# TensorE multiplies ones while the first weights are loaded and ahead of the first queries

## The chip, the cores and the metric

The kernel runs on one core of a Trainium2 chip. The metric is the device time of one execution in microseconds (us); smaller is better. Engines are named as in the profile: PE is TensorE's matmul, PEld its weight load, DVE is VectorE, ACT is ScalarE, POOL is GpSimd, SP is SyncE; a name with q (SPq, ACTq, PEq) is the queue or sequencer of that engine.

## The reference, cut to what matters

One layer of a gated cross-attention block, for 32 batches of 128 rows of 256 columns:

```python
xn  = layernorm(x)                                  # rows of 256
qh  = split_heads(xn  @ wq.T + wq_b)                # 16 heads of 16
kh  = split_heads(ctx @ wk.T + wk_b)
vh  = split_heads(ctx @ wv.T + wv_b)
att = softmax(qh @ kh.T / 4 + causal_mask) @ vh
x   = x + tanh(g_xattn) * (att @ dense_w.T + dense_b)
h   = layernorm(x)
e   = argmax(h @ router_w); p = softmax(h @ router_w)[e]      # 14 experts
x   = x + tanh(g_ffn) * p * (gelu(h @ w1[e] + b1[e]) @ w2[e] + b2[e])
```

## The kernel before, in words

The kernel has two stages. In the attention stage (up to about 320 us) it works as a software pipeline over batches: `run_steps` calls each engine's `step(t)` for t = 0 to 33, and in step t the engine works on several batches at once, at different depths. On PE, step t projects the keys of batch t-1 (`a1`) and transposes its normalised rows, projects the queries and values of batch t-2 (`a`), computes the scores of batch t-3 (`b`) and transposes its probabilities, and finishes batch t-4 (`c`). In the expert stage it goes through 45 tiles of 128 token rows, five buffers deep (`R = 5`): gather rows, transpose, multiply by `w1` of the tile's expert, GELU, multiply by `w2`, scatter.

Everything is ordered by hand with semaphores; each engine runs its own list in order. What matters here is the list of the first steps:

- SP's queue issues, in this order: x of batch 0, the first constants with the identity (L417), `wq` (L418), x of batch 1, the other constants (L420), `wv` (L421), the context of batch 1 (L422, issued at L385), `wd` (L423), the router's weights `rw` (L424), `wd_turned` (L425), then x and context of the next batches. ACT's queue issues the gates, the context of batch 0, `wk` (L719), and four small loads, the last of them `bd_column` (L723). All of these are asked for in the first 10 us, and `wk`, `wq`, `wv` are of 256 KB each.
- PE, step 1: wait for `wk` and the context of batch 0, project the keys of batch 0 (L1422), wait for the identity and the normalised rows, transpose them (L1506).
- PE, step 2: wait for `wq` (L1462), for the transposed rows (`xh_ready`, ACT L775) and the biased keys (`k_ready`, ACT L785), project the queries of batch 0 (L1422); wait for `wv`, project the values of batch 0 (L1489); wait for `q_ready` (DVE L1161) and the context of batch 1 (`c_loaded[1]`), project the keys of batch 1 (L1422); transpose its rows (L1506).
- PE, step 3 begins with a product for the output bias (L1431), which waits for `out_w_loaded` (`wd` and `rw`) and `bv_spread`. The latter comes from DVE's `cast_constants` (L846 to L857), which waits for the constants and the small loads and then runs L854 and L856. DVE's `fold_gate` (L859 to L864) follows on that product, and the first maxima of the scores on that.
- POOL begins with five memsets, L473 to L477: `half`, `values` (2048 columns), `seen`, `ones_bf` (a tile of ones, 128x128 bf16) and `ones`.

A matmul of two f32 tiles stands in the profile as two instructions: the projection of 256 rows of weights to 256 columns (2 halves, 2 chunks) is "x8". A value projection is "x4" of 256 columns. `bank[7]` is a PSUM bank; its first user before is the value projection of batch 0 (L1489), whose group of matmuls starts with `start=True`.

Of the kernel before, what the change touches and what calls it, by code (L numbers as in the profile page):

```python
# [7 lines left out]
P = 128  # L8
# [5 lines left out]
HQ = 4  # L14
# [94 lines left out]
def run_steps(eng, step):  # L109


    for t in range(12):
        step(Batch(0, t))
    with eng.Fori(3, B // 4 - 1) as i:
        for j in range(4):
            step(Batch(i, j))
    for t in range(B - 4, B + 2):
        step(Batch(t // 4, t % 4))
# [6 lines left out]
def flamingo_kernel(nc, x, ctxt, gates, wq, wk, wv, wd, wd_turned, bqk, bv, bd, bd_column, rw, w1b, w2, consts, out):  # L125
# [5 lines left out]
    with ExitStack() as ctx:  # L131
        def sb(name, shape, dt=F32):
            return ctx.enter_context(nc.sbuf_tensor(name, shape, dt))

        def sem(name):
            return ctx.enter_context(nc.semaphore(name))
# [14 lines left out]
        ones_bf = sb("ones_bf", [P, P], BF16)  # L151
# [103 lines left out]
        bank = [ctx.enter_context(nc.psum_tensor(f"bank{k}", [P, 512], F32)) for k in range(8)]  # L255
# [16 lines left out]
        c_loaded = [sem(f"c_loaded{r}") for r in range(4)]  # L272
        idle_written = sem("idle_written")
        setup_pool = sem("setup_pool")
        tanh_done = sem("tanh_done")
        consts_cast = sem("consts_cast")
        bv_spread = sem("bv_spread")
# [193 lines left out]
        @block.gpsimd  # L471
        def _(pool):
            pool.memset(half[:, :], -0.5)  # L473
            pool.memset(values, 0.0)
            pool.memset(seen[:, :], 0.0)
            pool.memset(ones_bf[:, :], 1.0)
            pool.memset(ones, 1.0)  # L477
            idle_row = g_out[:, 0:2, :].rearrange("p r d -> p (r d)")
            no_names = g_rows.rearrange("p r d -> p (r d)").bitcast(I32)[:, 0:NAMES // P * 2]
# [798 lines left out]
        def _(pe):  # L1278
# [71 lines left out]
            def transpose_probs(b, q):  # L1350
                pe.wait_ge(probs_ready, b.n * 4 + (q + 1))
                for v in range(HQ):
                    ins = pe.transpose(bank[4 + q % 2][:, v * P:(v + 1) * P], probs[:, q, v, :], ident)  # L1353
                ins.then_inc(probs_transposed, 1)
# [61 lines left out]
            def step(t):  # L1416
                a1, a, b, c, f = (t.back(k) for k in (1, 2, 3, 4, 6))

                def projected(at, w, src):
                    for half_ in range(DC):  # L1420
                        for ch in range(DC):
                            ins = pe.matmul(bank[6][:, at + half_ * P:at + (half_ + 1) * P],  # L1422
                                            w[:, ch, half_ * P:(half_ + 1) * P], src[:, ch, :],
                                            start=(ch == 0), stop=(ch == DC - 1))
                    return ins
# [33 lines left out]
                if a.ok():  # L1459

                    if a.static and a.n == 0:
                        pe.wait_ge(q_w_loaded, 16)  # L1462
                    pe.wait_ge(xh_ready, a.n + 1)
                    pe.wait_ge(k_ready, a.n + 1)
                    projected(0, wq_sb, xh_t[:, t.slot, :, :]).then_inc(q_done, 1)
# [16 lines left out]
                if a.ok():  # L1482
# [5 lines left out]
                    for ch in range(DC):  # L1488
                        ins = pe.matmul(bank[7][:, D:2 * D], c_in[:, a.slot, ch, :], wv_sb[:, ch, :],  # L1489
                                        start=(ch == 0), stop=(ch == DC - 1))  # L1490
# [17 lines left out]
                if b.ok():  # L1508
                    pe.wait_ge(probs_t_vector, b.n * 2 + 2)
                    transpose_probs(b, 3)  # L1510

            run_steps(pe, step)


# [127 lines left out]
```

## Time and profile before

| | us |
|---|---|
| median of 3 runs | 492.26 |
| lowest and highest of them | 491.57, 493.03 |
| profiled execution, its own time | 491.36 |
| span in the profile, first to last instruction | 489.5 |
| PE busy | 465.3 (95%) |
| first matmul starts at | 6.36 |

The busy time of PE is a sum over instructions that overlap in a pipeline, so it says where PE has work and not how fast it goes. The durations of equal instructions at different places say that. The strip called PEclk gives the granted clock of PE in 40 slices of the span. The chain of waits is the list of work that ended last, each piece released by the one before it.

### The profile page before, as it was taken

Reading aid. Unit: us, or ns where it says so; the run is one execution under the profiler, and the core shown is the slowest. Engines: PE = TensorE matmul, PEld = TensorE weight load, DVE = VectorE, ACT = ScalarE, POOL = GpSimd, SP = SyncE. Lnnn points to the kernel's source line nnn. Section 1 sums busy time; section 2 is a strip of 40 time slices with the busy share of each in tenths; the row PEclk is TensorE's granted clock in tenths of the full one; section 3 lists DMA queues with packets and bytes.
Section 4 is the critical chain, followed back from the end, with each engine's and each line's share of the span. In section 5 each row is a group of like instructions: output and inputs, shape, how many; then the busy total and the mean of one; then the engine's idle time right before and its main releaser. Section 6 shows DMA issues by size and latency. Waiting matters only on the chain.

```text
span 489.5 us, 17018 instructions
## 1 busy us (share of the span) xinstructions
PE 465.3 (95%) x4854; PEld 406.8 (83%) x4855; DVE 345.0 (70%) x1108; ACT 311.7 (64%) x1450; POOL 317.0 (65%) x686
## 2 busy tenths in 40 slices
PE   3999999999999999999999998989999999999991
PEld 3888888888888888888888887879899999999991
DVE  2778999999999999999999997654344334334431
ACT  1689899889898898898898897342222332233230
POOL 5385577786776777777777776685655555655621
PEclk9999999999999999999999999999999999999997
DMA  7274565312312212212211157598988888978810
GB/s 235 53 244 152 166 184 172 73 52 57 74 45 62 66 43 72 57 50 78 44 56 55 29 168 218 157 241 281 306 260 277 271 273 268 295 262 263 265 44 1
DMA packets 37904, 73.05 MB, mean 149 GB/s; under 512 B 12761, under 2 KB 21471, under 8 KB 37856
## 3 DMA queue, kind: packets, MB, share of 16 engines
q1 hardware_dynamic: 24752, 32.13, 23.2%
q10 hardware_dynamic: 6048, 23.54, 15.1%
q0 software_dynamic: 7056, 16.79, 11.2%
q8 instruction: 24, 0.39, 0.4%
q14 instruction: 24, 0.20, 0.2%
HBM read 59.06 MB, written 15.07 MB: 151 GB/s over the span
## 4 chain that ended last, share of the span: by engine, by line
PE 75%; ACT 7%; DVE 5%; DMA 4%; issue 3%; POOL 2%; ACTq 0%; POOLq 0%; DVEq 0%
PE bank L1322 14%; PE bank L1313 14%; PE bank L1422 10%; PE bank L1353 10%; ACT arena L759 7%; PE bank L1412 5%; PE bank L1489 5%; PE bank L1345 5%; PE bank L1361 4%; DMA g_rows<-token_rows,fetch_idx 3%; PE bank L1300 2%; PE bank L1408 2%; DVE negmax L981 2%; PE bank L1340 2%; PE bank L1402 1%
## 5 line engine op out<-in xcount | busy, mean ns | idle before, releaser
L759 ACT ACTIVATE arena<-bank,negmax 128x128 f32<-128x128 f32 x512 | 179.2, 400 | 13.5 <-DVE negmax L981 13.5
L743 ACT ACTIVATE hid_t<-bank,w_ring 128x128 f32<-128x128 f32 x180 | 51.2, 368 | 114.6 <-PE bank L1313 90.6
L759 ACT ACTIVATION_READ_ACCUMULATOR arena<-bank,negmax 128x1 f32 x512 | 123.4, 241 | 0.0
L981 DVE TENSOR_REDUCE negmax<-bank 128x4 f32<-128x512 f32 x128 | 84.6, 682 | 8.2 <-PE bank L1345 7.3
L1313 PE MATMUL bank<-g_xt,w_ring 128*128 128x128 f32 x720 | 87.9, 275 | 0.4 <-DVE g_xt L954 0.4
L1322 PE MATMUL bank<-W,hid_t 128*128 x360 | 85.5, 381 | 1.4 <-ACT hid_t L743 0.7
L1313 PEld LDWEIGHTS bank<-g_xt,w_ring 128*128 128x128 f32 x720 | 84.6, 192 | 1.4 <-issue 1.0
L970 DVE SCALAR_TENSOR_TENSOR g_out<-bank,g_name,g_out 128x256 f32<-128x256 f32 x45 | 21.8, 484 | 86.2 <-PE bank L1322 86.2
L1353 PE MATMUL bank<-C,arena 128*128 128x128 f32 x512 | 78.5, 276 | 2.4 <-ACT arena L759 1.8
L1422 PE MATMUL bank<-arena 128*128 128x128 f32 x512 | 72.8, 286 | 7.4 <-DMA arena<-wk 6.4
L1422 PEld LDWEIGHTS bank<-arena 128*128 128x128 f32 x512 | 63.8, 196 | 13.9 <-issue 7.7
L1322 PEld LDWEIGHTS bank<-W,hid_t 128*128 128x128 f32 x360 | 65.0, 190 | 9.4 <-issue 2.2
L1353 PEld LDWEIGHTS bank<-C,arena 128*128 128x128 f32 x512 | 60.1, 141 | 13.1 <-ACT arena L759 3.5
L542 POOL DMA_INDIRECT out<-g_out,g_name x45 | 44.8, 996 | 35.3 <-DVE g_out L963 16.0
L533 POOL DMA_INDIRECT g_rows<-token_rows,fetch_idx x45 | 45.5, 1012 | 31.2 <-POOL fetch_idx L531 28.2
L767 ACT ACTIVATE arena<-bank 128x512 f32<-128x512 f32 x64 | 40.8, 638 | 23.0 <-PE bank L1353 22.9
L512 POOL DMA_INDIRECT token_names<-name,pos x32 | 34.5, 1078 | 15.7 <-issue 13.0
L989 DVE COPY arena<-bank 128x512 f32<-128x512 f32 x64 | 43.7, 682 | 1.1 <-PE bank L1353 0.7
L559 POOL COPY arena<-rinv 128x128 f32<-128x128 f32 x64 | 17.1, 292 | 40.4 <-DVE rinv L1038 40.0
L521 POOL TENSOR_TENSOR arena<-arena,C 128x256 f32<-128x256 f32 x64 | 37.6, 605 | 1.9 <-ACT arena L785 1.9
L1412 PE MATMUL bank<-arena 128*128 128x270 f32 x128 | 37.1, 411 | 0.0
L508 POOL TENSOR_TENSOR rstd<-rstd,half 128x1 f32<-128x1 f32 x64 | 35.2, 558 | 0.6
(149 smaller groups left out, 765.9 us busy)
## 6 DMA issues: line engine op xcount, KB each, us to landing
w_ring<-w1b ACTq DMA_DIRECT2D x35, 642.0 KB, 5.0
token_rows<-rows SPq DMA_DIRECT2D x32, 256.0 KB, 3.7
W<-w SPq DMA_DIRECT2D x14, 512.0 KB, 5.6
w_ring<-w1b SPq DMA_DIRECT2D x10, 642.0 KB, 7.5
arena<-x SPq DMA_DIRECT2D x32, 128.0 KB, 2.0
arena<-ctxt SPq DMA_DIRECT2D x31, 128.0 KB, 3.1
slot_names<-token_names SPq DMA_DIRECT2D x45, 1.0 KB
g_rows<-token_rows,fetch_idx POOLq DMA_INDIRECT x45, 5.2
```

The costliest lines, as they stand in the source:

```text
L533: pool.indirect_dma_start(out=g_rows[:, r, :], out_offset=None, in_=source, in_offset=bass.IndirectOffsetOnAxis(ap=fetch_idx[:, r:r + 1], ...
L542: pool.indirect_dma_start(out=out_rows, out_offset=bass.IndirectOffsetOnAxis(ap=g_name[:, r, 0:1], axis=0), in_=g_out[:, r, :], in_offset= ...
L743: ins = act.activation(hid_t[:, RING[k], ch, :], hid_bank[k][:, ch * P:(ch + 1) * P], ACT.Gelu, bias=w_ring[:, k, B1_AT + ch:B1_AT + ch + 1])
L759: ins = act.activation(probs[:, q, v, :], bank[q][:, v * P:(v + 1) * P], ACT.Exp, bias=negmax[:, b.par, h:h + 1], accum_out=rsum[:, b.par, ...
L767: act.activation(probs_t[:, q, :, :].rearrange("p v s -> p (v s)"), bank[4 + q % 2][:, :], ACT.Copy).then_inc(probs_t_scalar, 1)
L981: dve.tensor_reduce(negmax[:, b.par, q * HQ:(q + 1) * HQ], bank[q][:, :].rearrange("p (v k) -> p v k", v=HQ), axis=AX_X, op=ALU.max, negat ...
L989: dve.tensor_copy(probs_t[:, q, :, :].rearrange("p v s -> p (v s)"), bank[4 + q % 2][:, :]).then_inc(probs_t_vector, 1)
L1313: ins = pe.matmul(hid_bank[r][:, f * P:(f + 1) * P], w_ring[:, r, at:at + P], g_xt[:, RING[r], ch, :], start=(ch == 0), stop=(ch == DC - 1))
L1322: ins = pe.matmul(y_bank[r][:, 0:D], hid_t[:, RING[r], ch, :], W2[:, bass.ds(ex, 1), ch, :].rearrange("p e n -> p (e n)"), start=(ch == 0) ...
L1353: ins = pe.transpose(bank[4 + q % 2][:, v * P:(v + 1) * P], probs[:, q, v, :], ident)
L1412: ins = pe.matmul(at[:, 0:WIDE], attn_t[:, ch * P:(ch + 1) * P], wd_sb[:, ch, :], start=(ch == 0), stop=(ch == DC - 1))
L1422: ins = pe.matmul(bank[6][:, at + half_ * P:at + (half_ + 1) * P], w[:, ch, half_ * P:(half_ + 1) * P], src[:, ch, :], start=(ch == 0), st ...
```

## The change: what it does

`ones_bf` is written second instead of fourth on POOL, and a semaphore `ones_written` tells of it. PE waits for it at its start and then issues 13 matmuls of that tile with itself: stationary 128x128 bf16 ones, moving 512 columns (the same 128 columns read four times), written over the whole of `bank[7]`, a result that nobody reads. In step 2, ahead of the wait for `wq` and the queries of batch 0, PE issues four more of them.

```diff
@@ semaphores
+        ones_written = sem("ones_written")
@@ gpsimd
             pool.memset(half[:, :], -0.5)
+            pool.memset(ones_bf[:, :], 1.0).then_inc(ones_written, 1)
             pool.memset(values, 0.0)
             pool.memset(seen[:, :], 0.0)
-            pool.memset(ones_bf[:, :], 1.0)
             pool.memset(ones, 1.0)
@@ tensor, step(t)
                     if a.static and a.n == 0:
+                        keep_warm(4)
                         pe.wait_ge(q_w_loaded, 16)
@@ tensor, before the steps
+            def keep_warm(n):
+
+                wide = ones_bf[:, :].rearrange("p (o k) -> p o k", o=1).to_broadcast([P, HQ, P])
+                for _ in range(n):
+                    pe.matmul(bank[7][:, :].rearrange("p (v k) -> p v k", v=HQ), ones_bf[:, :], wide,
+                              start=True, stop=True)
+
+            pe.wait_ge(ones_written, 1)
+            keep_warm(13)
             run_steps(pe, step)
```

## Rows read from the trace of the kernel before

**Rows 1.** The page's strip of granted clock, 40 slices of the span, in tenths.

```profile
PEclk9999999999999999999999999999999999999997
```

**Rows 2.** Busy time by engine in two stretches; columns named in the first line.

```profile
core 0: us, PE busy (x) PEld busy (x) DVE busy (x) ACT busy (x) POOL busy (x), PEclk, DMA share, GB/s
24.00:60.00 36.00, 36.00 (x457) 30.71 (x456) 30.41 (x90) 31.82 (x158) 23.11 (x62) 1.00 0.58 186
...
330.00:400.00 70.00, 68.78 (x476) 63.68 (x475) 26.75 (x73) 20.53 (x72) 41.48 (x58) 1.00 0.88 278
```

**Rows 3.** Chain of waits, first 16 us: start us, us, what.

```profile
1.65 4.66 DMA arena<-wk
...
6.36 2.08 PE bank L1422 x8
8.43 0.44 PE bank L1506 x2
...
9.18 0.63 ACT arena L785 x2
...
9.94 2.05 PE bank L1422 x8
11.99 1.48 PE bank L1489 x4
13.47 0.89 PE bank L1422 x8
14.36 0.22 PE bank L1506 x2
14.58 0.88 PE bank L1431 x4
...
15.48 0.43 DVE arena L861
```

**Rows 4.** Chain of waits later on: a value projection, and 16 bf16 matmuls.

```profile
30.82 0.87 PE bank L1489 x4
...
33.67 0.34 PE bank L1340 x16
```

**Rows 5.** Timeline of PE, value projection of batch 0: start us, us, instruction.

```profile
12.21 1.05 PE L1489 MATMUL bank<-arena 128*128 128x256 f32 x2
...
12.63 0.84 PE L1489 MATMUL bank<-arena 128*128 128x256 f32 x2
```

**Rows 6.** Timeline of POOL's memsets at the start.

```profile
0.74 1.80 POOL L474 MEMSET arena<- 128x2048 f32 x1
...
2.53 0.20 POOL L476 MEMSET ones_bf<- 128x128 bf16 x1
```

**Rows 7.** Timeline of the queues: issues of wv, context 1, bd_column, rw.

```profile
3.06 0.43 SPq L421 DMA_DIRECT2D arena<-wv  x1
...
3.54 0.43 SPq L385 DMA_DIRECT2D arena<-ctxt  x1
3.58 0.46 ACTq L723 DMA_DIRECT2D arena<-bd_column  x1
...
4.71 0.61 SPq L424 DMA_DIRECT2D arena<-rw  x1
```

**Rows 8.** DMA issues of these four: KB, us from issue to landing.

```profile
arena<-wv SPq DMA_DIRECT2D x1, 256.0 KB, 6.6
...
arena<-ctxt SPq DMA_DIRECT2D x1, 128.0 KB, 7.7
arena<-bd_column ACTq DMA_DIRECT2D x1, 1.0 KB, 7.9
...
arena<-rw SPq DMA_DIRECT2D x1, 14.0 KB, 7.5
```

**Rows 9.** Timeline of DVE in cast_constants, behind the small loads.

```profile
13.23 0.35 DVE L854 TENSOR_SCALAR g_rows<-arena,gate 128x256 f32<-128x256 f32 x1
...
13.49 0.29 DVE L856 COPY arena<-arena 128x256 f32<-128x256 f32 x1
```

**Rows 10.** Timeline of PE: its longest idle time after the start.

```profile
327.84 0.44 PE L1300 MATMUL bank<-C,g_rows 128*128 128x128 f32 x2 [1.37 <-DMA g_rows<-token_rows,fetch_idx]
```

## The prediction

> **What bounds the kernel now.** I read the chain of waits first, then the strip of granted clock, the stretches, and last the timelines and DMA issues of the first 16 us, where the whole change lies.
>
> The chain begins with a load: the keys' weights land at 1.65 + 4.66 = 6.31, and PE has nothing to do before. After that the chain is PE nearly throughout, with one turn over ACT (from the end of the transposes at 8.87 to the queries at 9.94, 1.07 us, of which 0.63 is ACT's two bias instructions) [rows 3]. The same code costs two prices there. The key projection at 6.36 takes 2.08 for 8 instructions, the query projection at 9.94 takes 2.05, but the key projection of the next batch, at 13.47, takes 0.89, all on the chain; the transposes fall from 0.44 to 0.22 [rows 3]. The value projection at 11.99 takes 1.48 for 4 instructions, and a later one 0.87 [rows 3, 4]. Its instructions start 0.42 us apart at 12.21 and 12.63, against 0.87 / 4 = 0.218 later [rows 4, 5]. A factor of two on equal instructions is TensorE's clock at its lower level, 1.2 GHz against 2.4. So PE runs at half rate from its first matmul at 6.36 to about 13.1 us, 6.7 us later, with one idle second in between. The strip of granted clock reads 9 in this first slice too [rows 1]; here I trust the durations and take the strip to show no more than that no later slice but the last fell.
>
> From 24 us on PE is busy 36.00 of 36.00 us, and in the expert stage 68.78 of 70.00 [rows 2]. What comes earlier into that stretch should come out earlier at the end.
>
> **The change, part by part.**
>
> *When the ones can start.* Their memset comes right behind that of `half`, so where the memset of `values` now starts, at 0.74, and takes 0.20 [rows 6]: 0.94, and PE starts at about 1.0. The memset of `values` moves back by that 0.20. The five memsets together take what they took and end before 3 us, while the first chain work is at 6.3, so I count nothing; if that cover were gone the price would be 0.2.
>
> *The price of one.* No bf16 matmul over the whole array and 512 columns is in the trace. From below: the 16 bf16 matmuls of 128 columns take 0.34, 0.021 each, so 512 columns 0.085 fast and 0.17 slow, and that with a quarter of the rows, four side by side [rows 4]. From above: an f32 instruction of 128 columns costs 2.05 / 8 = 0.256 slow and 0.89 / 8 = 0.111 fast, so 512 columns 1.02 and 0.445 [rows 3]. I take half of the f32 price per column, since the operand has half the bytes, from the value projections (256 f32 columns): 0.42 slow, 0.218 fast [rows 4, 5]. If those four side by side count as one, the bf16 row gives 4 x 0.34 / 4 = 0.34 fast and 0.68 slow, between my value and the upper end; rival 1 has its time.
>
> The Trainium skill (TensorE: Matmul & The Clock Gate, Back-to-back issue gap) gives the columns over 1.2 GHz for a slow matmul, an estimate of 0.427 us here and 13 x 0.427 = 5.55 us in all. By it the sum would be the same.
>
> *13 ahead of the keys.* 13 x 0.42 = 5.5, so slow throughout they end at 6.5. The weights land at 6.31 and the keys started at 6.36 [rows 3]: at most 0.15 late. If the clock rises on the way, they end earlier (9 slow and 4 fast: 5.7), hidden under the load altogether. At the low price they end at 3.2, and PE idles for 3 us before the keys.
>
> *Do they raise the clock in time?* In the trace the rise came 6.7 us after the first matmul, with a gap of 1.07 in it [rows 3]. The same distance from 1.0 gives 7.7 us; without a gap I expect it sooner. Take both ends, a rise by 6.4 and one at 7.7.
>
> *The path at the high clock.* Rise by 6.4: keys 6.45 to 7.4 (0.89, and I allow up to 0.2 more where they stand behind a wait), transposes 0.22 to 7.65, ACT's turn 1.07 to 8.7, queries 0.95 to 9.65. The values wait for `wv`, issued at 3.06 and landed 6.6 later, 9.66: just in time. They end at 10.55 (0.87) [rows 3, 4, 7, 8]. Then comes the wait that is late next: the keys of batch 1 need its context, issued at 3.54 and landed 7.7 later, at 11.24 [rows 7, 8]. Before it was hidden behind the slow work, since those keys started at 13.47 [rows 3]. So PE idles about 0.7 us and starts them at 11.3. Keys 0.89 to 1.09, transposes 0.22: 12.5. The bias product then needs `rw`, 4.71 + 7.5 = 12.21, and DVE's two instructions behind `bd_column`, 3.58 + 7.9 = 11.48 and 0.55 for the two, 12.03 [rows 7 to 9]: both just ready. It takes 0.88 and ends at 13.3 to 13.4, where it ended at 15.46 [rows 3].
>
> The sum: 15.46 - 13.35 = 2.1 us, bounds 1.9 and 2.3. PE's own arithmetic would give more: 1.1 on the keys, 0.22 on the transposes, 1.1 on the queries, 0.6 on the values are 3.0; the load of context 1 keeps 0.7 to 0.9 of it.
>
> Rise at 7.7: keys at 6.5, until 7.7 4.7 of 8 slow, the rest in 0.37, end 8.1; transposes 8.3, queries 9.4 to 10.3, values to 11.2. The keys of batch 1 start at 11.3 all the same. The idle 0.7 us takes up the late rise, and the sum stays 2.1.
>
> *The 4 ahead of the queries.* They start at 7.65 and take 4 x 0.218 = 0.87 in ACT's turn of 1.07: hidden, 0.2 to spare. With the clock slow they take 1.7 and push the queries by 0.6; with the upper price 1.78 and 0.7. Both still fit in the 0.7 us ahead of the context, if nothing else is late. Behind them on PE stands everything of the chain. What they fill is a second of idleness; the longest idle time in the trace behind the start, 1.37 us, stands in a strip that reads 9 on both sides, and the work behind it is at the fast price (0.44 for two overlapping transposes) [rows 1, 10]. So I count no gain for them.
>
> *Bank 7.* PE alone writes it before the first value projection, in its own order: no wait added. The one added wait, for the ones, has an idle engine behind it.
>
> *Afterwards.* From the bias product on the loads are in or are issued relative to the steps. PE full means that the 2.1 us stay [rows 2]. The transfer of each step then collides with the same work as before.
>
> **The time.** The profiled execution took 491.36 (span 489.5): 491.36 - 2.1 = 489.3. The median shown is 492.26, 0.9 above it, which gives 490.2. I forecast 489.9: the moment of the rise is not a piece of the program, the profiled execution may have had an early one, and the runs before spread over 1.46 us (491.57 to 493.03). If a part of that spread is a later rise in those runs, the change takes it away too.
>
> The Trainium skill (TensorE: Matmul & The Clock Gate, the part on the clock gate) says outright that the moment of the rise varies between executions of one kernel, and that the ramp costs less than 1% of a typical span. By the first, the gain on the median is larger than the trace's 2.1, up to 2.9 (time 489.4), and the runs after stand closer together; one trace can't show it. By the second, less than 4.9 us, a bound the 3.0 above agrees with.
>
> **Rivals.**
>
> 1. *The price is high.* Each of the 13 costs 1.02 slow and 0.445 fast, as the f32 rows do [rows 3]. With a rise at 7.7, 6.5 are done by then and the other 6.5 take 2.9: the keys start at 10.6, end at 11.5, the transposes at 11.7, four more to 13.5, queries 14.4, values 15.3, keys 16.2, transposes and bias product 17.3 instead of 15.46: +1.85, 493.2 by the profiled execution and 494.1 by the median. It is slower by over 0.3% from about 0.9 us each. With 0.68 and 0.34 the same walk ends at 15.2, 0.25 ahead of before. Against it: bf16 rows are cheaper than f32 ones in the trace [rows 4].
> 2. *Ones don't count as work for the clock.* The rise stays at 13.1 or comes later. Keys start 0.15 late, the four cost 1.7 less the turn, together +0.8 at the queries; part of the values run fast afterwards: +0.4 at the bias product, 491.8 to 492.7, no change that can be told, slower if the rise moves too. Nothing in the trace speaks for it.
> 3. *The gain is real and smaller.* The rise is later than 7.7, or a load of the first 12 us lands later, the context, `rw` or `bd_column`, which were all hidden and are within 0.3 us of the new path [rows 7 to 9]. A rise at 9.5 costs the four dummies slow and a slow start, queries 10.1 to 11, values 11.9, some 0.6 past the context: gain 1.5. A load 1 us late: gain 1.1 to 1.3. That gives 490.8 to 491.3.
> 4. *It is not carried.* The 2.1 us are taken back where PE meets something with its own time, the gathers with their 1.37 us wait [rows 10]. Time 491.5 to 492.3. Against it: that gather is issued behind POOL's own work of the same pipeline, which moves with it.
>
> **Chances.** Forecast (a gain of 1.5 to 3 on the median) 0.73; rival 3 0.13; rival 4 0.06; rival 2 0.04; rival 1 0.03; something unnamed 0.01. A measurement of this kernel can tell about 0.3%, 1.5 us, from no change; faster means below 490.8. Faster: nearly all of the forecast and a little of rival 3, 0.74. Same: the rest of 3, rival 4, most of 2, 0.21. Slower: rival 1 and the rest of 2, 0.05. The range goes from 488.9 (the median's gain of 2.9 and 0.5 for what the runs spread) to 491.5 (rival 3 and the beginning of rival 4).
>
> **What the next profile would show.** PE's first matmul at 1.0, 13 of them 0.42 apart, some perhaps 0.22 apart at the end. First keys at 6.4 to 6.6, at about 1.0 instead of 2.08. Queries at 8.7, and a first chain row of DMA for the context of batch 1 with an idle PE of 0.5 to 0.8 before the keys at 11.3. Bias product ended by 13.5, every later row 2.1 earlier, to the last scatter. The forecast is wrong if the keys start after 7, if queries still cost 2.05, if the key projection of batch 1 starts after 12, or if the shift of 2.1 at 24 us is gone at 480.

## The result, and the profile after

| | before | changed |
|---|---|---|
| median, us | 492.78 (13 runs) | 490.32 (13 runs) |
| lowest, highest | 490.88, 496.83 | 488.41, 491.46 |
| profiled execution, its own time | 491.36 | 491.46 |

The ratio is 0.9942, with a 95% interval of 0.9924 to 0.996: faster by 0.4% to 0.8%, 2.5 us between the medians. The forecast was 489.9, in 488.9 to 491.5. But the profiled execution of the changed kernel is no faster than that of the kernel before, and it was the slowest of its 13. Its trace shows what can still go wrong.

The chain of waits of the changed kernel, start us, us, what (line numbers are 1 more than before, 2 more behind L1464):

```profile
3.54 7.92 DMA arena<-ctxt
...
11.60 1.13 PE bank L1423 x8
12.73 0.22 PE bank L1508 x2
12.95 0.88 PE bank L1432 x4
...
19.38 0.63 PE bank L1354 x4
20.00 1.91 PE bank L1491 x4
21.92 0.85 PE bank L1354 x4
22.77 1.36 PE bank L1423 x8
```

It no longer begins with the keys' weights [rows 3] but with the context of batch 1, as the walk had it: issued at 3.54, the keys of batch 1 behind it. The bias product (L1432) ends at 13.83, where it ended at 15.46 [rows 3]: 1.63 us earlier. Then, from 20.0, a value projection costs 1.91, transposes 0.85 and a key projection 1.36. At the same place in the chain of the kernel before they cost 1.13, 0.44 and 0.89:

```profile
21.63 1.13 PE bank L1489 x4
22.76 0.44 PE bank L1353 x4
23.20 0.89 PE bank L1422 x8
```

The difference of the three is 1.66 us. The timeline of PE in the trace of the changed kernel, with the idle time before an instruction in brackets:

```profile
1.00 5.71 PE L1518 MATMUL bank<-ones_bf 128*128 128x512 bf16 x13 [1.00 <-POOL ones_bf L475]
6.68 1.16 PE L1423 MATMUL bank<-arena 128*128 128x128 f32 x8
7.68 0.38 PE L1508 MATMUL bank<-C,arena 128*128 128x128 f32 x2
7.90 1.03 PE L1518 MATMUL bank<-ones_bf 128*128 128x512 bf16 x4
9.14 1.13 PE L1423 MATMUL bank<-arena 128*128 128x128 f32 x8 [0.22 <-ACT arena L786]
10.17 1.13 PE L1491 MATMUL bank<-arena 128*128 128x256 f32 x4
11.60 1.13 PE L1423 MATMUL bank<-arena 128*128 128x128 f32 x8 [0.29 <-DMA arena<-ctxt]
...
18.38 0.52 PE L1383 MATMUL bank<-arena 128*128 128x14 f32 x4
18.74 0.60 PE L1385 MATMUL bank<-arena,g_rows 128*128 128x14 f32 x4
```

The 13 start at 1.00; keys and queries cost 1.16 and 1.13 where they cost 2.08 and 2.05 [rows 3]. The clock was up by the first key. Busy time by engine in four stretches of this trace (columns as in rows 2; the number behind POOL's is the granted clock):

```profile
13.40:16.80 3.40, 3.40 (x50) 2.70 (x50) 2.78 (x7) 0.96 (x5) 1.81 (x4) 1.00 0.07 20
16.80:20.20 3.40, 2.88 (x23) 2.48 (x23) 3.03 (x10) 3.40 (x21) 1.76 (x3) 1.00 0.39 103
20.20:23.60 3.40, 3.40 (x13) 2.94 (x13) 1.58 (x6) 2.42 (x12) 1.14 (x5) 0.50 0.17 49
23.60:27.00 3.40, 3.40 (x69) 2.69 (x71) 0.89 (x2) 1.88 (x7) 1.22 (x4) 1.00 0.81 302
```

From 20.2 to 23.6 PE runs at the lower level, 1.2 GHz. Before it lies a stretch with little matmul work: instructions of 14 columns (the router's weights folded with others, L1373 to L1385), transposes, and half a microsecond of idleness. 3.4 us at half rate hold 1.7 us of work at the full rate, so 1.7 us are lost, as the three rows above say; that is about what had been won. The first steady score step (batch 1, L1341) starts in this trace and in that of before at:

```profile
24.78 0.33 PE bank L1341 x16
```

```profile
24.75 0.33 PE bank L1340 x16
```

So the profiled execution won 1.6 us by 14 us and gave it back by 24. The kernel before passed the same code at full clock in its profiled execution. Was the fall part of the change, or chance? And what do the 13 and the 4 each do?

### The profile page after: what moved, and what is told of

The parts are those of the page before. It is cut to its first block, busy times and chain, and to the rows that moved or that the text cites. A ratio compares the mean times of both kernels' runs of the same rounds, so it can differ in the third digit from the quotient of the medians.

```text
span 489.6 us, 17052 instructions
## 1 busy us (share of the span) xinstructions
PE 471.0 (96%) x4871; PEld 408.1 (83%) x4872; DVE 344.8 (70%) x1108; ACT 312.6 (64%) x1450; POOL 317.3 (65%) x686
## 4 chain that ended last, share of the span: by engine, by line
PE 74%; ACT 7%; DVE 5%; DMA 4%; issue 3%; POOL 2%; SPq 1%; ACTq 0%; POOLq 0%; DVEq 0%
PE bank L1323 14%; PE bank L1314 14%; PE bank L1354 10%; PE bank L1423 9%; ACT arena L760 7%; PE bank L1413 5%; PE bank L1346 5%; PE bank L1491 5%; PE bank L1362 4%; DMA g_rows<-token_rows,fetch_idx 3%; PE bank L1301 2%; PE bank L1409 2%; DVE negmax L982 2%; PE bank L1341 2%; DMA arena<-ctxt 2%
## 5 line engine op out<-in xcount | busy, mean ns | idle before, releaser
L971 DVE SCALAR_TENSOR_TENSOR g_out<-bank,g_name,g_out 128x256 f32<-128x256 f32 x45 | 21.8, 484 | 86.5 <-PE bank L1323 86.5
L1423 PE MATMUL bank<-arena 128*128 128x128 f32 x512 | 71.5, 283 | 0.5 <-DMA arena<-ctxt 0.3
L1423 PEld LDWEIGHTS bank<-arena 128*128 128x128 f32 x512 | 62.7, 193 | 8.5 <-issue 7.0
```

## The experiments

The theory: the 13 lift the half-rate start; the stretch near 20 us is a second place where the clock may fall, in this kernel and in the kernel before. The rivals stand in the expectations. The runs came in three sessions; each run is compared with the kernel before of its own session. In the first, everything was slower (before 500.48), in the other two before took 492.66 and 493.05. A ratio is not the quotient of the two medians; in the second session the two differ by up to 0.2%.

**The changed kernel again**, unchanged.

> The changed kernel once more. Theory (clock): the 13 multiplications raise TensorE's clock before the first keys in every execution, and the work up to the scores of batch 0 ends 1.6 to 2.1 us earlier; but the stretch with little matmul work that follows (16.8 to 20.2 us in the first trace of the changed kernel) lets the clock fall in some executions, at 1.7 us a time. So the times fall into two groups, about 488.5 to 489.6 and 490.3 to 491.5, and a trace has either the half-rate stretch near 20 us and ends like the kernel before, or has none and ends 1.6 to 2.9 us earlier. Rival (the loss is a fixed one): every trace of this kernel has the half-rate stretch at 20.2 us, and the two groups come from elsewhere, for example the gathers.

Measured: 497.45 against 500.48, ratio 0.9943 (0.9925 to 0.9961). The times spread over 3.4 us without two clean groups, so that part missed. The trace has the fall at 20 us again (columns as above), so the rival of a fixed loss is not out by it:

```profile
20.00:23.40 3.40, 3.38 (x12) 2.93 (x13) 2.34 (x7) 2.67 (x16) 0.37 (x2) 0.50 0.11 39
```

It shows something not expected too: the keys' weights landed 6.12 us after their issue, not 4.66 [rows 3], and the keys started at 7.82 with PE idle for 1.2 us behind the ones. The bias product ended at 14.47, 1.0 us earlier than in the trace of before and not 1.6 to 2.1.

**Only the 13.**

```diff
                     if a.static and a.n == 0:
-                        keep_warm(4)
                         pe.wait_ge(q_w_loaded, 16)
```

> The 13 ahead of the keys are kept, the 4 ahead of the queries are left out. Theory (the 13 do it all): the queries of batch 0 still take about 1.0 us and start at 9.1, since the idle 1.3 us ahead of them is too short for the clock to fall; time equal to the changed kernel within 0.5 us. Rival (the 4 hold the clock): the queries or what follows take the double, and up to 1.5 us of the gain is lost, time 490.5 to 492.

Measured: 497.06, ratio 0.9939 (0.9916 to 0.9961), the same as the changed kernel in that session. The timeline of PE:

```profile
1.00 4.58 PE L1517 MATMUL bank<-ones_bf 128*128 128x512 bf16 x13 [1.00 <-POOL ones_bf L475]
6.55 1.16 PE L1423 MATMUL bank<-arena 128*128 128x128 f32 x8 [0.97 <-DMA arena<-wk]
...
9.02 1.13 PE L1423 MATMUL bank<-arena 128*128 128x128 f32 x8 [1.08 <-ACT arena L786]
```

The queries cost 1.13 after 1.08 us of idleness. The four bought nothing here, as forecast. This trace has no fall near 20 us.

**Only the 4.**

```diff
-            keep_warm(13)
             run_steps(pe, step)
```

> The 13 ahead of the keys are left out, the 4 ahead of the queries are kept. Theory (the 13 do it all): the keys take 2.08 us from 6.36, the 4 run at half rate, 1.7 us, and push the queries of batch 0 from 9.94 to 10.8; the clock rises at some moment between 9.9 and 13.2, since the idle second is filled. Time from 0.8 us slower than before to 1 us faster. Rival (filling the idle second alone is enough): clock up by 10, time as the changed kernel.

Measured: 498.21, ratio 0.9961 (0.994 to 0.9981). That is 2.3 us below before by the medians, more than the 1 us that was expected at most; its interval overlaps those of the other two, so by time alone it can't be set apart from them. The chain:

```profile
7.78 2.04 PE bank L1423 x8
9.82 0.43 PE bank L1508 x2
10.25 1.71 PE bank L1518 x4
11.95 1.28 PE bank L1423 x8
13.23 0.86 PE bank L1491 x4
```

Keys at half rate, the four at half rate on the chain (1.71, of which ACT's turn would have taken 1.07), then queries partly at the full rate: 1.28 is 0.39 more than 0.89, so half rate until about 12.7. The half rate lasts 5 us from the first key at 7.78, less than the 6.7 and more of the kernel before; the four pay about 0.6 us for that. The rival's mechanism, clock up by 10, is not in this trace. Nor is the gain: it is of the slowest of the 12 executions, its weights landed at 7.68, and its bias product ended at 16.29. Where the gain of the median comes from stays open.

**Three fillers in the thin stretch.** They multiply into bank 4, which is not yet in use, and stand where PE waits for the first probabilities.

```diff
                 if b.static and b.n == 0:
                     fold_router()
+                    keep_warm(3, bank[4])
```

> The changed kernel, and 3 more multiplications of ones (into bank 4, not yet in use) between the folding of the router and the first transposes of probabilities in step 3, where TensorE is idle for 0.5 to 0.75 us. Theory (clock falls for want of matmul work in that stretch): fewer executions or none fall to half rate near 20 us; the times gather at 488.5 to 489.6, median about 1 us below the changed kernel's. Rival (they are too few, or it is not idleness that counts): the same two groups as the changed kernel. The cost of the 3 is nothing up to 0.2 us at the transposes.

Measured: 496.36, ratio 0.9929 (0.9903 to 0.9955), 1.1 us below the changed kernel of that session by the medians, with intervals that overlap; again in the last session, see below. No fall near 20 us in the trace; this is a lead, not a proof.

**The kernel before again.**

> The kernel before, unchanged, for a second trace of it. Theory (the moment of the rise and the falls differ between executions): the first matmul is at 6.3 to 7.9, the keys and queries of batch 0 run at half rate, and the clock rises at another moment than 13.1 us, between 11 and 16.5; the bias product (L1431) ends between 15 and 17.5 us. Rival (the rise is a fixed time after the first matmul): it comes 6.7 us after it.

Measured: 492.74 against 492.66, ratio 1.0013 (0.999 to 1.0037). Its trace answers the question of chance. First the chain, then the stretches of the fall and before it:

```profile
9.92 2.04 PE bank L1422 x8
11.97 1.71 PE bank L1489 x4
13.67 1.57 PE bank L1422 x8
15.25 0.22 PE bank L1506 x2
15.47 0.88 PE bank L1431 x4
```

```profile
18.00:21.80 3.80, 3.31 (x31) 3.18 (x29) 3.38 (x9) 2.95 (x17) 2.84 (x6) 1.00 0.25 73
21.80:25.20 3.40, 3.37 (x13) 2.87 (x13) 2.42 (x7) 2.75 (x16) 0.30 (x2) 0.50 0.12 39
```

The values cost 1.71, all slow, and the keys of batch 1 1.57, not 0.89 [rows 3]: 0.68 too much is 1.36 us of half rate, from 13.67 to about 15.0. That is 8.7 us after the first matmul at 6.34, not 6.7. The fixed distance is refuted. And the kernel before has the fall as well, over the same instructions, from 21.8 to 25.2. The first profiled execution of before had the earlier rise of the two and no fall.

**14 columns in place of 512**, in the 13 and in the 4.

```diff
-                wide = ones_bf[:, :].rearrange("p (o k) -> p o k", o=1).to_broadcast([P, HQ, P])
                 for _ in range(n):
-                    pe.matmul(bank[7][:, :].rearrange("p (v k) -> p v k", v=HQ), ones_bf[:, :], wide,
+                    pe.matmul(bank[7][:, 0:14], ones_bf[:, :], ones_bf[:, 0:14],
```

> The changed kernel with every multiplication of ones cut from 512 columns to 14: as many instructions and weight loads at the same places, hardly any columns. Theory (what raises the clock is the array's work, not that instructions run): the 13 end by 2.5 us, the keys and queries of batch 0 take 2.0 to 2.1 us each as before, time as the kernel before, 0 to 0.5 us faster. Rival (any early instruction starts the ramp, or the gain is from the earlier memset): time as the changed kernel, 0.6% less than before.

Measured: 492.11, ratio 1.0004 (0.9982 to 1.0027): no change. The timeline:

```profile
1.00 0.51 PE L1517 MATMUL bank<-ones_bf 128*128 128x14 bf16 x13 [1.00 <-POOL ones_bf L475]
7.01 2.08 PE L1423 MATMUL bank<-arena 128*128 128x128 f32 x8 [5.49 <-DMA arena<-wk]
```

Same instructions, same start, same weight loads, done after 0.51 us: the keys are back at 2.08. The gain comes from 5 us of multiplying, not from early instructions nor from the earlier memset.

**The context of batch 1 first** (on top of the fillers), and later **the same without the fillers**.

```diff
+            load_c(Batch(0, 1))
+            sp.dma_start(wv_sb, wv).then_inc(v_w_loaded, 16)
             sp.dma_start(C[:, FIRST_CONSTS:], consts[:, FIRST_CONSTS:]).then_inc(consts_loaded, 16)
-            sp.dma_start(wv_sb, wv).then_inc(v_w_loaded, 16)
-            load_c(Batch(0, 1))
```

> The changed kernel with the 3 fillers of step 3, and the context of batch 1 issued ahead of wv and of the second constants. Theory (the context of batch 1 holds the keys of batch 1): it lands 1 to 2 us earlier, these keys start by 11.0 instead of 11.5 and wait for TensorE's own work or for wv; the bias product then waits for rw or bd_column and ends at 13.1 to 13.4 instead of 13.73: 0.3 to 0.6 us at most. Rival (the queues are full, so another load takes its place): wv or rw lands later by as much, and the bias product ends at 13.7 or later.

Measured: 488.57, ratio 0.9934 (0.9906 to 0.9962), eight runs from 487.65 to 489.77, a spread of 2.1 us and all below the median of before. The chain:

```profile
6.41 1.16 PE bank L1423 x8
7.57 0.23 PE bank L1509 x2
...
8.87 1.13 PE bank L1423 x8
9.99 0.87 PE bank L1492 x4
10.86 1.07 PE bank L1423 x8
11.93 0.22 PE bank L1509 x2
12.15 1.01 PE bank L1432 x4
```

PE goes from the values straight to the keys of batch 1, and the bias product ends at 13.16. With the fillers alone and the old order of the loads it ended at 13.62 (trace of the last session, keys at 6.21 there): the load had held at least 0.46 us, as the theory had it. No fall near 20 us in this trace.

> The changed kernel with the context of batch 1 issued ahead of wv and of the second constants, without the fillers. Theory (two separate effects): the bias product ends near 13.2 instead of 13.8 us, 0.4 to 0.6 us less, but the fall near 20 us stays possible and the spread stays at 3 us; median 0.3 to 0.7 us below the changed kernel's. Rival (the order of the loads made the low and narrow times of the run with both): times as there, 487.6 to 489.8 on a chip where the kernel before takes 492.7.

Measured: 488.59 against 493.05, ratio 0.9914 (0.9889 to 0.9938), five runs from 488.11 to 489.75. The bias product ends at 13.06, as the theory has it; the trace has the fall, from 18.4 to 21.8, and this execution was the slowest of the five. The rest of the theory missed: the spread is 1.6 us and not 3, and the median is 1.6 us below the changed kernel's of the same session (490.15, below) and not 0.3 to 0.7. By its times the rival fits better: they lie in its 487.6 to 489.8 without any filler. So by times nothing shows that the fillers add to the earlier context; five runs with one fall among their traces can't decide it.

**The fillers without the 13 and the 4.**

> Neither the 13 nor the 4: only the 3 fillers of step 3 (and the earlier memset of the ones). Theory (two effects): the half-rate start stays, keys and queries of batch 0 at 2.05 us; a fall of the clock near 20 us, where the kernel before has one in some executions, is rarer. Time between the kernel before and 1 us less. Rival (the fall, not the start, is what costs): most of the 0.6% of the changed kernel is already here.

Its edit is the filler above with both `keep_warm(13)` and `keep_warm(4)` left out. Measured: 491.39, ratio 0.9991 (0.9967 to 1.0015). No fall in the trace, keys and queries at 2.04 and 2.05, the keys of batch 1 at 1.31 from 13.59, so a rise at about 14.4. By the medians it is 1.3 us below before, by the ratio 0.1%, with up to 0.33% inside the interval, against 0.58% for the changed kernel. The rival, that most of the gain would already be here, is unlikely by that and not excluded; the trace shows that the half-rate start is not touched.

**The changed kernel a third time, and the fillers again**, side by side in the last session.

> The changed kernel a third time, to stand beside the next two on one chip. Theory (a fall near 20 us in some executions): times in two groups, 1.5 to 2 us apart, ratio to the kernel before 0.994 to 0.995. Rival (one group): a spread below 1.5 us.

Measured: 490.15, ratio 0.9946 (0.9923 to 0.9968); seven runs, four from 489.04 to 490.15, two at 491.23 and 491.50, and the profiled one at 492.79. The spread of 3.75 us puts the rival out; the two groups are not clean by time alone, but see the mean clock below. The profiled one shows a third way to lose (timeline, and stretches):

```profile
1.00 4.74 PE L1518 MATMUL bank<-ones_bf 128*128 128x512 bf16 x13 [1.00 <-POOL ones_bf L475]
7.78 1.88 PE L1423 MATMUL bank<-arena 128*128 128x128 f32 x8 [2.04 <-DMA arena<-wk]
9.45 0.63 PE L1508 MATMUL bank<-C,arena 128*128 128x128 f32 x2
9.88 1.80 PE L1518 MATMUL bank<-ones_bf 128*128 128x512 bf16 x4
```

```profile
8.00:11.40 3.40, 3.40 (x14) 2.51 (x14) 0.99 (x3) 0.90 (x3) 1.03 (x3) 0.50 0.93 312
```

The clock rose early, so the 13 were over at 5.74; the weights came late, at 7.74; PE idled for 2.04 us and the clock fell at 8.0. Keys and the four at half rate, the four now on the chain, bias product at 15.62, later than the 15.46 of the first trace of before. But that trace of before had its weights at 6.31. With only the 4, and weights at 7.68, the bias product ended at 16.29, 0.67 us later than here, so some gain may be left; the kernel before with late weights is in no trace. This trace had the fall near 21.7 as well.

> The changed kernel with the 3 fillers of step 3, again. Theory (the fillers keep the clock up near 20 us): no half-rate stretch there, times only in the lower group, median 0.8 to 1.5 us below the changed kernel's on this chip, ratio to the kernel before about 0.992. Rival (the first trace without a fall was luck): the median stands within 0.4 us of the changed kernel's and the times are spread as widely.

Measured: 489.08, ratio 0.9926 (0.9902 to 0.9951), five of six runs from 488.48 to 489.14 and one at 490.74. Against the changed kernel that is 1.1 us by the medians, but each ratio lies inside the other's interval, so the difference is not shown. Where the changed kernel idles, the timeline now has the fillers, and the stretch after stays at 1.00:

```profile
17.06 0.81 PE L1519 MATMUL bank<-ones_bf 128*128 128x512 bf16 x3
```

```profile
20.20:23.60 3.40, 3.40 (x50) 3.07 (x52) 1.39 (x5) 2.76 (x13) 1.33 (x6) 1.00 0.40 99
```

Over all traces: of ten traces without the fillers seven show a fall in this stretch (the changed kernel in all three of its traces, before in one of two), of four with them none. With four traces, an effect of the fillers is likely and not shown.

The record has one thing more, the mean granted clock of every execution. In the traces outside the first session it is 0.988 to 0.992 with such a fall and 0.992 to 0.995 without (below 1 there too, since every trace ends at half rate, as the 7 in rows 1 shows for before). Of the 13 executions of the changed kernel in the result, three have 0.994 or 0.995 and took 488.62 to 489.03; four have 0.991 or less and took 490.32 to 491.46; the six at 0.992, which can be either, lie anywhere between 488.41 and 491.25. With the 14 columns, five at 0.995 took 490.74 to 491.62 and five at 0.991 or less 492.60 to 494.07. So the fall is there in some executions and not in others, at close to 2 us a time, and the rival of a fixed loss is out.

**Zeros for ones.**

```diff
-            pool.memset(ones_bf[:, :], 1.0).then_inc(ones_written, 1)
+            pool.memset(zeros_bf[:, :], 0.0).then_inc(ones_written, 1)
+            pool.memset(ones_bf[:, :], 1.0)
```

(and `zeros_bf` in place of `ones_bf` in `keep_warm`).

> The changed kernel with a tile of zeros multiplied with itself in place of the tile of ones, same shapes and places. Theory (the clock follows the columns streamed, not their values): clock up before the keys, keys and queries at 1.1 us each, time as the changed kernel. Rival (it follows switching in the array, and zeros switch nothing): keys and queries at 2.05 us each, time as the kernel before.

Measured: 489.90, ratio 0.9937 (0.9913 to 0.9961). Keys 1.16, queries 1.13:

```profile
6.31 1.16 PE L1425 MATMUL bank<-arena 128*128 128x128 f32 x8 [0.65 <-DMA arena<-wk]
```

Zeros do what ones do, so the rival is out. What matters is the multiplying of 512 columns for 5 us against 14 columns for half a microsecond; whether it is the columns or the time that they take, these two runs don't separate.

**One number for the rest.** The time of a profiled execution less the start of the scores of batch 1 in its trace says what the whole rest costs. The start is the chain's row of L1340 (L1341 or L1343 where lines moved); these are worked out from it:

| | time | start of these scores | rest |
|---|---|---|---|
| before | 491.36 | 24.75 | 466.61 |
| before, again | 492.64 | 26.99 | 465.65 |
| changed | 491.46 | 24.78 | 466.68 |
| changed, third | 492.79 | 26.50 | 466.29 |
| fillers, again | 489.14 | 22.92 | 466.22 |
| fillers and context | 488.58 | 22.47 | 466.11 |
| context alone | 489.75 | 23.62 | 466.13 |
| fillers alone | 491.52 | 25.28 | 466.24 |
| 14 columns | 491.62 | 25.28 | 466.34 |
| zeros | 489.90 | 23.57 | 466.33 |

The start moves over 4.5 us and the rest stays within 1.1, seven of ten within 0.3. What is won before 24 us is kept to the end. In the first session the rest was 473.65 to 474.33, and all four traces there have one long wait near 325 us, of 4.1 to 4.9 us, with a fall during it or right behind it. The changed kernel's, again:

```profile
329.45 0.77 PE L1314 MATMUL bank<-g_xt,w_ring 128*128 128x128 f32 x2 [4.84 <-DVE g_xt L955]
```

against 0.20 us at the same wait in the first trace of before. The rest is over 7 us longer in all four kernels traced in that session; what made it so stays open, and the comparisons within the session don't depend on it.

## Why the prediction was right

The direction and the time hold: 489.9 forecast, 490.32 measured, a gain of 2.4 us forecast and 2.5 measured. The mechanism at the start holds too: the 14 columns in place of 512 take the whole gain away. That the number comes so near is in part luck. The trace gave 1.63 us at the bias product where 2.1 was forecast, and nothing was left of it at 24 us; the median gained more than that, most likely because other executions of the kernel before start worse than its first profiled one, which the forecast had put in as a guess of 0.3 us. By its steps:

- *When the ones can start*: 0.94 and 1.0 forecast, 1.00 found, at no price for POOL.
- *The price of one*: 0.42 slow and 0.218 fast. The 4 took 1.03, which is 4 x 0.218 and 0.16 for the end of the last; the 13 took 5.71, less 0.16 that is 0.427 each. Right, and rival 1 is out.
- *13 ahead of the keys*: at most 0.15 late was forecast. Keys at 6.68 instead of 6.36, 0.3 late, and the weights came last: these landed 5.0 us after their issue and not 4.66, at about 6.65. Where they landed at about 6.35 (the first trace with the 3 fillers), the keys started at 6.53 behind the 13, 0.17 late, close to the forecast. The landing of `wk` was taken as a constant; it came between 6.2 and 7.8 us in the 14 traces. A late landing after an early rise brought half rate back for the keys (changed, third). No rival had this.
- *Do they raise the clock in time?* Yes: keys at 1.16 to 1.20 in eight of nine traces with the 13; in the ninth it was up before them and fell again. That the rise comes at different moments was a guess for the kernel before and is now seen: about 13.1, 15.0, 13.6 and 14.4 us in the four traces that began like the kernel before (both of before, the 14 columns, the fillers alone), 6.6 to 8.7 us after the first projection's start. The Trainium skill (TensorE: Matmul & The Clock Gate, Part 1) says that the moment varies from run to run, by about 500 ns to either side. These traces agree that it varies, and their spread, 2.1 us in the distance from the first projection, is wider.
- *The path at the high clock*: the context of batch 1 as the next wait was right, at 11.46 for 11.24. The sum was 2.1 with bounds 1.9 and 2.3 and measured 1.63 (15.46 to 13.83), outside the bounds. The mis-sized terms: the keys of batch 1 started at 11.60 for 11.3, since the context landed 7.92 after its issue and not 7.7, and what follows to the end of the bias product took 2.23 (1.13, 0.22, 0.88) for 2.05. The loads had been given no spread. The steps ahead of that were late as well, the queries at 9.14 for 8.7, and the values at 10.17, as `wv` landed 7.1 us after its issue and not 6.6; the wait for the context hid this, but left PE idle for 0.29 us and not 0.5 to 0.8.
- *The 4 ahead of the queries*: hidden and worth nothing where the 13 did their work: as said. In the third trace of the changed kernel they stood on the chain.
- *Afterwards*: "PE full means that the 2.1 us stay". This is the step that failed in the profiled execution. The sentence looked at 24 us and later, where it is right (table above), and passed over 16 to 24, where PE is busy in the rows but with few columns. The shift was gone at 24.78 for 24.75, by 3.4 us at half rate from 20.2. Rival 4 placed the loss at the gathers; it was at 20 us.
- *The signs of being wrong* that the forecast named did come in two of the three traces of the changed kernel: keys at 7.82 and 7.78, after 7, and the keys of batch 1 at 12.28 and 13.43, after 12. In both the late weights made them, not a clock that stayed down ahead of the keys.
- *The time*: 0.9 between profiled execution and median put down in part to a later rise. That fits: the first profiled execution of before had the earliest rise of the four above and no fall. It is the likely reason why 2.5 us of gain on the median stand above 1.6 in the trace. The runs of the changed kernel were expected to stand closer together: in the result they do (3.05 against 5.95 us from lowest to highest), in the last session they don't (3.75 against 3.33).

The gain of the median is, as I read it, a sum over cases; no run measures their shares. Half-rate start removed: 1.63 us against a rise at 13.1, 2.52 against one at 15.0 (the bias product ended at 16.35 in the second trace of before, at 13.83 in the changed kernel's first). Falls near 20 us, 1.7 us each, come in both kernels and so should cancel on average; whether the change makes them more frequent (three of three traces against one of two) stays open.

## What to carry to other kernels

Where PE waits for its first weights, give it multiplications of 512 columns that depend on one small memset, for about the time until the weights can land (here 4.6 to 5.7 us for the 13). Take that time from several traces: in two of the nine traces with them PE stood idle for 1.2 and 2.0 us behind the ones, and in one they held the keys for 0.17 us. No run tried more or fewer than 13, so where the best number lies is not shown. Then look for the next load in the queue, since it takes over the chain, and for thin stretches behind it: here half a microsecond of idleness among instructions of 14 columns and transposes was followed by half rate in seven of ten traces. And judge such a change by many runs: the first profile of each kernel alone would have said that nothing was gained.

## What was not expected of the hardware

- With a tile of zeros the keys cost 1.16 us, as with one of ones; with 14 columns in place of 512 they cost 2.08.
- Idle times of 1.08 us (only the 13) and 1.22 us (changed, again) left the clock up, 2.04 us (changed, third) were followed by a fall.
- A fall need not follow a long wait: ahead of the one at 20.2 us PE was busy 2.88 of 3.40 us in the rows, mostly with 14-column work and transposes, and its longest idle time was 0.49 us.
- The 256 KB of `wk`, issued at 1.65 or 1.66 each time, landed after 4.5 to 4.7 us in eight traces, 4.9 and 5.0 in two, 5.3 in one and 6.0 to 6.1 in three.
